# One pass of matmuls for values and row sums in a perceiver block: halves aligned by small transfers, the product moved to other engines, the mask spread by TensorE

## The chip, the cores and the metric

The kernel runs on one core of a Trainium2 chip. The metric is the time of one execution on the device in microseconds (us). The engines are PE (TensorE; PEld is its weight load), DVE (VectorE), ACT (ScalarE), POOL (GpSimd) and SP (SyncE, which here only issues transfers). Each runs its own instructions strictly in order; they meet through semaphores.

## The reference

64 sequences of 64 queries, model width 128, 16 heads of 8. Only the first 64 of the 128 context rows count, because of the causal mask. Three layers, each added to x:

```python
# layer one: cross attention on layernorm(x), keys and values from ctx
scores = einsum('bhqd,bhkd->bhqk', Q, K) / sqrt(8); scores = where(mask == 0 or k > q, -inf, scores)
x = x + softmax(scores) @ V, heads joined, @ Wo
# layer two: self attention on layernorm(x), keys and values through a latent of 32
scores = clip(q k / sqrt(128), -1e4, 1e4) * exp(-1e-4 * |q - k|)
x = x + softmax(scores) @ V, heads joined, @ Wo
# layer three: feed-forward on layernorm(x), 128 -> 512 -> 128, GELU, inputs and weights rounded to 127 steps
```

## The kernel before

A **tile** is 128 rows of x: two sequences of 64 queries. There are 32 tiles (`NT`) in each attention layer, numbered 0 to 31 in layer one and 32 to 63 in layer two (`NS` = 64). The program is a software pipeline written out by hand: each engine has its own loop over **turns** n, and in turn n an engine works on tile n for the early steps and on older tiles for the late ones. `due(n, lags)` says which tile a step has in turn n. The order inside a turn is the order of the lines in each engine's loop, and an engine that waits holds up all that stands behind the wait.

In turn n of layer one:

- PE: `scores(n)` (L560) into four banks of PSUM (the accumulators); `values` of tile n-3, which is 16 small matmuls with the values as weights (L606, numerator) and then 8 with a table of ones (L612, the sums of the exponentials, spread over the same partitions); `project` of tile n-4 (L622, with Wo); `to_keys(n-2)`, eight transposes in two halves (L579); then one "piece", mostly a projection of four tiles (kinds q, k, v, x; L474, L487, L495, L458). fp32 matmuls other than transposes show as two instructions each.
- DVE: scale the scores and add the mask (L1027); `add_residual` of tile n-4 (L962), which waits for `project`; the row maxima (L1046); `divide` of tile n-3 (L968), the product of numerator and inverse sum, which gives `oT`, the input of `project`; moments for a later layernorm (L938, L942).
- POOL: subtract the maxima (L408, 128x1024); later in layer one also a normalisation (`normalise`, L329).
- ACT: logarithm of the sum (L834), exponentials of tile n-2 in two halves (L829) with the inverse of the sum, exp(-log), between them (L840), then the copy of the piece out of PSUM (L786, L778, L797, L772).

In layer two the lags of `values` and `project` are one turn longer; DVE clips (L1032) and takes maxima in two halves (L1041, L1043); POOL multiplies by the decay (L400, 128x1024) and subtracts the maxima of half the heads (L408, 128x512); PE subtracts the other half itself (`shift_keys`, L591), into the bank of the second half of the transposes, whose exponential ACT takes first in the next turn.

The banks for `project`, the transposes and the pieces form a ring of three (`NR`), in the order of the list `order`: who comes three places later waits until the bank has been read. Numerator and sums share the bank `OB`. Every fourth turn SP spreads new keys over `kx` with four transfers (L305). The mask is loaded for all 128 partitions and made by POOL in eight groups (`make_mask`, L364 and L367).

## Time and profile before

| | |
|---|---|
| median of 3 runs | 310.81 us (310.68 to 311.25) |
| the profiled execution | 311.19 us, span of the profile 309.4 us |
| busy: PE, DVE, ACT, POOL | 285.5, 255.9, 219.6, 209.9 us |
| first and last L1027 (layer one) | 10.1 and 129.0 us |
| first and last L1032 (layer two) | 132.8 and 252.2 us |

Layer one and layer two take the span from about 10 to 260 us, and layer three the rest. An engine's busy time says how full it is; which of the engines sets the length of a turn is read from waits and from the order of the instructions.

### The profile page before, as it was taken

To read this page: it belongs to the slowest core of one execution; us is meant where nothing else is said; L and a number is where in the kernel's file an instruction comes from. 1 tells how busy PE (TensorE), PEld (TensorE's weight loads), DVE (VectorE), ACT (ScalarE), POOL (GpSimd) and SP (SyncE) were. 2 spreads that over 40 slices of the span, in tenths; PEclk is the share of its full clock that TensorE was granted. 3 is DMA by queue.
4 is the path that set the end of the run, shared out by engine and by line. 5 is a ranking of instruction groups with operands and counts; after the bars stand their busy time and mean duration, and the time that the engine had idled before them with its cause. 6 is when DMAs were issued, how large, how long until landed. Compare 5 with 4: busy or idle time off the path is not lost.

```text
span 309.4 us, 13624 instructions
## 1 busy us (share of the span) xinstructions
PE 285.5 (92%) x5744; PEld 197.6 (64%) x5744; DVE 255.9 (83%) x558; ACT 219.6 (71%) x496; POOL 209.9 (68%) x167
## 2 busy tenths in 40 slices
PE   7789879999999999999999999999999999699593
PEld 2356547676767777675767686777777768332282
DVE  2898679999888888888888787878888998789873
ACT  3585856575768876666777778788857877699590
POOL 5676557777877766799999998988799962230000
PEclk9999999999999999999999999999999999999869
DMA  8999000101010000000000000000000000000027
GB/s 229 313 286 298 12 28 4 36 2 40 2 37 9 31 19 20 28 14 24 17 33 6 21 20 21 19 21 20 11 31 5 2 5 4 0 0 0 2 78 195
DMA packets 19038, 15.05 MB, mean 49 GB/s; under 512 B 5985, under 2 KB 15522, under 8 KB 18978
## 3 DMA queue, kind: packets, MB, share of 16 engines
q1 hardware_dynamic: 18258, 13.75, 15.5%
q8 instruction: 46, 0.75, 1.1%
q10 hardware_dynamic: 720, 0.43, 0.5%
q14 instruction: 14, 0.11, 0.1%
HBM read 8.67 MB, written 2.10 MB: 35 GB/s over the span
## 4 chain that ended last, share of the span: by engine, by line
PE 73%; DVE 15%; issue 4%; DMA 3%; ACT 2%; POOL 1%; SPq 1%; DVEq 0%; ACTq 0%; POOLq 0%
PE ps L579 12%; PE ps L560 11%; PE ps L606 10%; PE ps L612 8%; PE ps L622 8%; DVE hmax L1108 6%; PE ps L577 4%; PE ps L495 4%; PE ps L487 4%; PE ps L474 3%; PE ps L591 3%; DVE u L1027 3%; PE ps L718 2%; DMA arena<-in_mask_BxS_if 2%; DMA out<-pt 1%
## 5 line engine op out<-in xcount | busy, mean ns | idle before, releaser
L829 ACT ACTIVATE pt<-ps 128x512 f32<-128x512 f32 x128 | 76.0, 595 | 30.5 <-PE ps L579 23.3
L408 POOL TENSOR_TENSOR u<-u,mx 128x1024 f32<-128x1024 f32 x32 | 60.8, 1902 | 35.3 <-DVE mx L1046 35.1
L400 POOL TENSOR_TENSOR ud<-u,con 128x1024 f32<-128x1024 f32 x31 | 73.4, 2367 | 6.6 <-DVE u L1032 6.5
L1027 DVE SCALAR_TENSOR_TENSOR u<-ps,rs,arena 128x1024 f32<-128x1024 f32 x32 | 40.9, 1279 | 14.1 <-PE ps L560 12.7
L1032 DVE TENSOR_SCALAR u<-ps 128x1024 f32<-128x1024 f32 x32 | 39.0, 1220 | 11.8 <-PE ps L560 11.3
L560 PE MATMUL ps<-arena,qT 32*64 32x256 f32 x1024 | 44.0, 399 | 4.9 <-DVE u L1027 2.5
L606 PE MATMUL ps<-pt,vx 128*32 128x64 f32 x2048 | 41.4, 221 | 2.9 <-DVE oT L968 1.3
L606 PEld LDWEIGHTS ps<-pt,vx 128*32 128x32 f32 x2048 | 32.5, 110 | 16.4 <-issue 11.5
L612 PE MATMUL ps<-pt,con 128*32 128x128 f32 x1024 | 40.0, 273 | 0.7 <-issue 0.7
L1046 DVE TENSOR_REDUCE mx<-u 128x16 f32<-128x1024 f32 x32 | 38.7, 1210 | 0.1
L834 ACT ACTIVATE lden<-ps 128x128 f32<-128x128 f32 x64 | 17.7, 277 | 29.5 <-PE ps L612 29.4
L560 PEld LDWEIGHTS ps<-arena,qT 32*64 32x64 f32 x1024 | 14.9, 129 | 31.2 <-issue 21.6
L579 PE MATMUL ps<-con,u 128*128 128x128 f32 x256 | 33.3, 273 | 0.0
L408 POOL TENSOR_TENSOR ud<-ud,mx 128x512 f32<-128x512 f32 x30 | 31.3, 1043 | 2.4
L622 PE MATMUL ps<-wo,oT 128*128 128x128 f32 x128 | 31.3, 326 | 0.7 <-DVE oT L968 0.7
L938 DVE BATCH_NORM_STATS2 stats<-x 128x6 f32<-128x128 f32 x96 | 25.7, 280 | 5.4 <-DMA x<-in_x 5.2
L579 PEld LDWEIGHTS ps<-con,u 128*128 128x128 f32 x256 | 28.9, 141 | 0.6 <-issue 0.6
L622 PEld LDWEIGHTS ps<-wo,oT 128*128 128x128 f32 x128 | 19.0, 188 | 13.3 <-issue 12.1
L962 DVE TENSOR_TENSOR x<-ps,x 128x128 f32<-128x128 f32 x64 | 18.5, 290 | 10.7 <-PE ps L622 10.5
L797 ACT COPY vx<-ps 64x256 f32<-64x256 f32 x64 | 23.4, 366 | 4.9 <-PE ps L495 4.0
L612 PEld LDWEIGHTS ps<-pt,con 128*32 128x32 f32 x1024 | 25.9, 110 | 1.0 <-issue 1.0
L1041 DVE TENSOR_REDUCE mx<-u 128x8 f32<-128x512 f32 x32 | 21.6, 676 | 0.2
(153 smaller groups left out, 513.5 us busy)
## 6 DMA issues: line engine op xcount, KB each, us to landing
arena<-kT SPq DMA_DIRECT2D x52, 64.0 KB, 2.2
out<-pt SPq DMA_DIRECT2D x8, 256.0 KB, 2.8
arena<-in_ctx_cols SPq DMA_DIRECT2D x4, 256.0 KB, 4.5
xn3T<-in_x_cols SPq DMA_DIRECT2D x4, 256.0 KB, 4.6
x<-in_x SPq DMA_DIRECT2D x4, 256.0 KB, 5.2
arena<-in_ctx_cols SPq DMA_DIRECT2D x2, 512.0 KB, 6.3
xn3T<-in_x_cols SPq DMA_DIRECT2D x2, 512.0 KB, 6.0
x<-in_x SPq DMA_DIRECT2D x2, 512.0 KB, 7.3
```

The source lines that it names most:

```text
L400: pool.tensor_tensor(dh, uh, decay.unsqueeze(1).to_broadcast([P, H, HALF]), ALU.mult)\
L408: pool.tensor_tensor(uh, uh, mx[:, n % 4, 0:count].unsqueeze(2).to_broadcast([P, count, HALF]), ALU.subtract)\
L560: last = pe.matmul(ps[HALF * b:HALF * (b + 1), r].rearrange("p (h k) -> p h k", h=HR)[:, :, 0:HALF], qT[rows, j % RING3, i * P + HALF * b: ...
L579: last = pe.transpose(out_t, in_t, ident)
L606: pe.matmul(ps[32 * r:32 * (r + 1), bank, HALF * b:HALF * (b + 1)], vx[:, j % RING3, b, i, r].rearrange("p c m -> p (c m)")[:, 16 * par:16 ...
L612: last = pe.matmul(ps[32 * r:32 * (r + 1), bank, P:2 * P], ones[:, par], pt[:, n % 2, 2 * r + par, :], start=(par == 0), stop=(par == 1))
L622: pe.matmul(ps[:, bank, 0:D], oT[:, n % 2], wo[:, layer], start=True, stop=True)\
L829: act.activation(pt[:, n % 2, 4 * half:4 * half + 4].rearrange("p h n -> p (h n)"), ps[:, bank, :], ACT.Exp).then_inc(s["emptied"], 1)
L938: dve.bn_stats(stats[:, k, t % 4], x[:, t]).then_inc(ST[k], 1)
L1027: dve.scalar_tensor_tensor(by_head(u[:, n % UB]), sc, rs[:, 0, n:n + 1], mask[:, n].unsqueeze(1).to_broadcast([P, H, HALF]), ALU.mult, ALU ...
L1032: dve.tensor_scalar(by_head(u[:, n % UB]), sc, CLAMP, -CLAMP, ALU.min, ALU.max)\
L1046: dve.tensor_reduce(mx[:, n % 4], by_head(u[:, n % UB]), AX.X, ALU.max)\
```

## The change

`values` no longer runs its second set of 8 matmuls (L612), except in the last two tiles. The weights of the first set become 32 columns wide with values and ones in turn, so that 16 matmuls give numerator and sum together: in one half of the bank the numerators stand on even partitions and the sums on odd ones, in the other half the reverse (the last two tiles keep the old way with weights of their own, `vl`). So that numerator and sum stand on the same partition, ACT copies the bank out (`take_out`, 128x256 into `raw`), and SP starts four transfers between partitions for each tile (`align`, 64 partitions x 512 bytes each, `raw` to `nd`). The logarithm of a tile waits for its two transfers `D_IN`, the product for `N_IN`, and both come one turn later than before (`LAG_DEN`), as do `project` and `add_residual`. `values` waits for the copy of the tile before (`raw_done`), no longer for its product.

The product of tiles 0 to 31 is made by POOL, behind the subtraction of its turn; that of tiles 32 to 61 by DVE, with the inverse sum in PSUM. The mask is loaded for two partitions only, made into bf16 by DVE, and spread and joined with the causal part by PE (piece `m`, 8 tiles at a time, copied out by ACT). The ones in the weights are set once, by DVE and POOL at the start. Some turns of layer three's layernorm move by one.

```diff
+LAG_T, LAG_SHIFT, LAG_PV, LAG_DEN = 2, 3, (3, 4), (4, 5)
+WHOLE = NS - 2
+def den_turn(n):
+    return n + (LAG_PV[1] if n >= WHOLE else LAG_DEN[n // NT])
+def divided(turn):
+    return [n for n in range(NS) if den_turn(n) == turn]
+def added(turn):
+    return [n for n in range(NS) if den_turn(n) + 1 == turn]
...
+        def product_made(eng, n):
+            eng.wait_ge(s["o_first" if n < NT else "o_ready"], n % NT + 1)
...
+            def align(n):
+                slot = n % RAW
+                sp.wait_ge(s["raw_done"], n + 1)
+                if n >= RAW:
+                    product_made(sp, n - RAW)
+                sp.dma_start(nd[0:P:2, slot, 1], raw[1:P:2, slot, 0]).then_inc(D_IN[slot], 16)
+                sp.dma_start(nd[1:P:2, slot, 1], raw[0:P:2, slot, 1]).then_inc(D_IN[slot], 16)
+                sp.dma_start(nd[0:P:2, slot, 0], raw[0:P:2, slot, 0]).then_inc(N_IN[slot], 16)
+                sp.dma_start(nd[1:P:2, slot, 0], raw[1:P:2, slot, 1]).then_inc(N_IN[slot], 16)
...
 # POOL, behind the subtraction of turn n
-                for m, (turn, _, _, _) in enumerate(MAKE):
-                    if turn == n:
-                        make_mask(m)
+                for tile in divided(n):
+                    if tile < NT:
+                        divide(tile)
...
 # PE
                 if 1 <= n < NS - 1:
-                    pe.wait_ge(s["o_ready"], n)
+                    pe.wait_ge(s["raw_done"], n)
+                if NT + 2 <= n < NS - 1:
+                    product_made(pe, n - 2)
+                if n < WHOLE:
+                    for b in range(2):
+                        for par in range(2):
+                            for r in range(RG):
+                                last = pe.matmul(ps[32 * r:32 * (r + 1), bank, P * par + HALF * b:P * par + HALF * (b + 1)],
+                                                 vx[:, j % RING3, b, i, r, 32 * par:32 * (par + 1)],
+                                                 pt[:, n % 2, 2 * r + par, HALF * b:HALF * (b + 1)], start=True, stop=True)
+                    last.then_inc(s["pv_done"], 1)
+                    return
...
 # ACT
+            def take_out(n):
+                act.wait_ge(s["pv_done"], n + 1)
+                if n >= RAW:
+                    act.wait_ge(D_IN[n % RAW], aligned(n - RAW))
+                    act.wait_ge(N_IN[n % RAW], aligned(n - RAW))
+                act.copy(raw[:, n % RAW].rearrange("p a n -> p (a n)"), ps[:, OB, 0:2 * P])\
+                    .then_inc(s["raw_done"], 1)
+
             def log_den(n):
-                act.wait_ge(s["pv_done"], n + 1)
-                act.activation(lden[:, n % 2], ps[:, num_den(n), P:2 * P], ACT.Ln).then_inc(s["ln_done"], 1)
+                if n < WHOLE:
+                    act.wait_ge(D_IN[n % RAW], aligned(n))
+                    act.activation(lden[:, n % 2], nd[:, n % RAW, 1], ACT.Ln).then_inc(s["ln_done"], 1)
...
 # DVE
+            dve.wait_ge(s["mask_in"], 16)
+            dve.tensor_scalar(mask_b[:, :], mask_i, 0.0, MASKED, ALU.is_equal, ALU.mult).then_inc(s["mask_cast"], 1)
             for t in range(GT):
                 moments(0, t)
...
-                for tile in due(n, LAG_ADD):
+                for tile in added(n):
                     add_residual(tile)
...
-                for tile in due(n, LAG_PV):
-                    if tile not in (EARLY, NS - 1):
+                for tile in divided(n):
+                    if NT <= tile < NS - 1:
                         divide(tile)
```

Three places of the new order follow. First POOL, around turns 15 to 18 of layer one. Before, behind the splitting of a bias:

```order
L346 CAST b2h<-b2d 1x128 [waits b2_split]
L408 TENSOR_TENSOR u<-u,mx 128x1024 [waits maxed] x3
L329 TENSOR_SCALAR xn3T<-x,mv,rs 128x128 [waits rs1]
L408 TENSOR_TENSOR u<-u,mx 128x1024 [waits maxed]
L329 TENSOR_SCALAR xn3T<-x,mv,rs 128x128 [waits rs1]
```

And now (`nd` lies in the tensor arena; L480 is the subtraction, L406 the product):

```order
L427 CAST b2h<-b2d 1x128 [waits b2_split]
L480 TENSOR_TENSOR u<-u,mx 128x1024 [waits maxed]
L406 TENSOR_TENSOR oT<-arena,rden 128x128 [waits wo_done,n_in0,den_ready]
L480 TENSOR_TENSOR u<-u,mx 128x1024 [waits maxed]
L406 TENSOR_TENSOR oT<-arena,rden 128x128 [waits wo_done,n_in1,den_ready]
L480 TENSOR_TENSOR u<-u,mx 128x1024 [waits maxed]
L406 TENSOR_TENSOR oT<-arena,rden 128x128 [waits wo_done,n_in2,den_ready]
L410 TENSOR_SCALAR xn3T<-x,mv,rs 128x128 [waits rs1]
```

A product stands behind each subtraction; the one in turn n is that of tile n-4. Second DVE, one turn of layer one (scores, addition of tile n-4, maxima, product of tile n-3, moments) before:

```order
L1027 SCALAR_TENSOR_TENSOR u<-ps,rs,arena 128x1024 [waits s_done,rs0,filled]
L962 TENSOR_TENSOR x<-ps,x 128x128 [waits wo_done]
L1046 TENSOR_REDUCE mx<-u 128x16 [waits s_read]
L968 TENSOR_TENSOR oT<-ps,rden 128x128 [waits wo_done,den_ready]
L938 BN_STATS stats<-x 128x6 [waits mv1,x_added]
L942 BN_AGGR mv<-stats 128x2 [waits st1]
```

And now:

```order
L1156 SCALAR_TENSOR_TENSOR u<-ps,rs,arena 128x1024 [waits s_done,rs0,filled]
L1086 TENSOR_TENSOR x<-ps,x 128x128 [waits wo_done]
L1175 TENSOR_REDUCE mx<-u 128x16 [waits s_read]
L1062 BN_STATS stats<-x 128x6 [waits mv1,x_added]
L1066 BN_AGGR mv<-stats 128x2 [waits st1]
```

The product is gone from DVE, and the addition, now of tile n-5, still stands ahead of the maxima. Third ACT, one turn of layer one before:

```order
L834 ACTIVATE lden<-ps 128x128 [waits pv_done]
L829 ACTIVATE pt<-ps 128x512 [waits pv_done,filled]
L840 ACTIVATE rden<-lden 128x128 [waits o_ready,ln_done]
L829 ACTIVATE pt<-ps 128x512 [waits filled]
L846 ACTIVATE w1r<-w1r,cst,scal 128x512 [waits wscale]
```

And now:

```order
L946 ACTIVATE lden<-arena 128x128 [waits d_in1]
L940 COPY arena<-ps 128x256 [waits n_in2,d_in2,pv_done]
L932 ACTIVATE pt<-ps 128x512 [waits pv_done,filled]
L956 ACTIVATE rden<-lden 128x128 [waits o_first,ln_done]
L932 ACTIVATE pt<-ps 128x512 [waits filled]
```

The logarithm of one tile, which waits for transfers, now stands ahead of the copy that starts the transfers of the next.

## Rows read from the trace of the kernel before

**Rows 1.** The page's busy times and its chain that ended last.

```profile
PE 285.5 (92%) x5744; PEld 197.6 (64%) x5744; DVE 255.9 (83%) x558; ACT 219.6 (71%) x496; POOL 209.9 (68%) x167
...
PE 73%; DVE 15%; issue 4%; DMA 3%; ACT 2%; POOL 1%; SPq 1%; DVEq 0%; ACTq 0%; POOLq 0%
```

**Rows 2.** Busy time in stretches: layer one, then four turns of layer two.

```profile
50.00:80.00 30.00, 29.70 (x611) 20.80 (x599) 29.09 (x72) 18.93 (x53) 24.10 (x27) 1.00 0.06 21
...
165.54:181.35 15.81, 15.77 (x378) 11.46 (x376) 13.19 (x34) 11.97 (x30) 14.69 (x11) 1.00 0.07 21
```

**Rows 3.** Timeline of layer two: ACT, PE and PEld in one turn.

```profile
182.56 0.60 ACT L829 ACTIVATE pt<-ps 128x512 f32<-128x512 f32 x1 [0.38 <-PE ps L591]
182.79 0.61 PE L612 MATMUL ps<-pt,con 128*32 128x128 f32 x16
183.33 0.49 PE L622 MATMUL ps<-wo,oT 128*128 128x128 f32 x2
183.54 0.47 PEld L579 LDWEIGHTS ps<-con,ud 128*128 128x128 f32 x4
...
185.51 0.23 PEld L560 LDWEIGHTS ps<-arena,qT 32*64 32x64 f32 x16
```

**Rows 4.** Groups by line: busy, mean ns, idle before.

```profile
L612 PE MATMUL ps<-pt,con 128*32 128x128 f32 x1024 | 40.0, 273 | 0.7 <-issue 0.7
L797 ACT COPY vx<-ps 64x256 f32<-64x256 f32 x64 | 23.4, 366 | 4.9 <-PE ps L495 4.0
L387 POOL TENSOR_TENSOR wkv_raw<-wkv_raw 128x128 f32<-128x128 f32 x1 | 0.5, 463 | 0.0
```

**Rows 5.** Timeline of layer one: PE, DVE and POOL in one turn.

```profile
99.71 0.49 PE L622 MATMUL ps<-wo,oT 128*128 128x128 f32 x2
100.24 0.29 DVE L962 TENSOR_TENSOR x<-ps,x 128x128 f32<-128x128 f32 x1
100.45 1.21 DVE L1046 TENSOR_REDUCE mx<-u 128x16 f32<-128x1024 f32 x1
101.74 1.90 POOL L408 TENSOR_TENSOR u<-u,mx 128x1024 f32<-128x1024 f32 x1 [1.12 <-DVE mx L1046]
103.63 0.79 POOL L329 TENSOR_SCALAR xn3T<-x,mv,rs 128x128 f32<-128x128 f32 x1
```

**Rows 6.** Timeline of DVE: the additions of turns 8 and 31.

```profile
44.00 0.29 DVE L962 TENSOR_TENSOR x<-ps,x 128x128 f32<-128x128 f32 x1
...
130.29 0.29 DVE L962 TENSOR_TENSOR x<-ps,x 128x128 f32<-128x128 f32 x1
```

**Rows 7.** Timeline of POOL: decays of turns 35, 36, 40, 41 and 62.

```profile
147.35 2.37 POOL L400 TENSOR_TENSOR ud<-u,con 128x1024 f32<-128x1024 f32 x1
150.80 2.38 POOL L400 TENSOR_TENSOR ud<-u,con 128x1024 f32<-128x1024 f32 x1
...
165.08 2.38 POOL L400 TENSOR_TENSOR ud<-u,con 128x1024 f32<-128x1024 f32 x1
169.01 2.37 POOL L400 TENSOR_TENSOR ud<-u,con 128x1024 f32<-128x1024 f32 x1
...
250.06 2.37 POOL L400 TENSOR_TENSOR ud<-u,con 128x1024 f32<-128x1024 f32 x1
```

**Rows 8.** Key transfers: issue time and time to landing, at 84 and 99 us.

```profile
L305 SPq DMA_DIRECT2D arena<-kT x4: 459/594/1687, 84.1 to 86.9; - x4
DMA to landing us min/median/max: 1.9/2.6/3.0
...
DMA to landing us min/median/max: 1.8/1.9/1.9
```

**Rows 9.** Timeline of the start: what the first scores wait for.

```profile
7.57 1.41 DVE L1012 TENSOR_SCALAR arena<-kT,con 128x512 f32<-128x512 f32 x3
7.92 1.32 POOL L364 TENSOR_SCALAR arena<-arena 128x256 f32<-128x256 int32 x1 [3.26 <-DMA arena<-in_mask_BxS_if]
10.11 1.28 DVE L1027 SCALAR_TENSOR_TENSOR u<-ps,rs,arena 128x1024 f32<-128x1024 f32 x1 [1.12 <-POOL arena L367]
```

More of the change, by code:

```diff
@@ L104, in ring_plan @@
         pieces[n] += these
+    for c in range(1, NT // MASK_TILES):
+        pieces[MASK_TURN[c]].append(("m", c))
     for n in range(NS):
@@ L116, in ring_plan @@
         keys = [("t", turn - LAG_T, half) for half in range(2)] if 0 <= turn - LAG_T < NS else []
-        order += [("o", n) for n in due(turn, LAG_ADD)] + keys + pieces[turn]
+        order += [("o", n) for n in added(turn)] + keys + pieces[turn]
         by_act += [("t", n, 1) for n in [turn - LAG_SHIFT] if NT <= n < NS] + (keys if turn - LAG_T < NT else keys[:1]) + pieces[turn]
@@ L224, in perceiver_block @@
         KX_IN = [s[f"kx_in{n}"] for n in range(RING3)]
-        MASK_IN = [s[f"mask_in{n}"] for n in range(4)]
+        N_IN, D_IN = [s[f"n_in{n}"] for n in range(RAW)], [s[f"d_in{n}"] for n in range(RAW)]
         STORED = [s[f"stored{n}"] for n in range(4)]
@@ L261, in gelu_count, with aligned, columns_of @@
             return 1 + max(m for m, e in enumerate(GELUS) if e[0] == k)
+        def aligned(n):
+            return 32 * (n // RAW + 1)
+        def columns_of(v, slot, e, first, between):
+            pitch, blocks = v.shape[1] * v.shape[2] * v.shape[3] * RG * VW, v.shape[3] * RG
+            return [bass.AP(v[:, :, :, :, :, :].tensor, HALF * e * pitch + (2 * slot + b) * blocks * VW + 2 * DH * e + first,
+                            [[pitch, HALF], [VW, blocks], [between, 2], [2, DH]]) for b in range(2)]
         def gets_empty(what):
@@ L772, in piece @@
                     last = act.copy(xT[:, j % 2], ps[:, bank, :])
+                if kind == "m":
+                    last = act.copy(mask[:, j * MASK_TILES:(j + 1) * MASK_TILES].rearrange("p t k -> p (t k)"), ps[:, bank, :])
                 if kind == "cq":
@@ L1033, in _ @@
                         .then_inc(s["clipped"], 1)
-                for tile in due(n, LAG_ADD):
+                for tile in added(n):
                     add_residual(tile)
@@ L1160 @@
             a = a[:, spread]
+        if name in _OF_VALUES:
+            a = a[by_turns]
         a = _np.ascontiguousarray(a)
```

196 lines of the change are left out of this document (128 added, 68 removed).

## The prediction

> **What bounds the kernel now.** I read the page first: PE is busy 92% of the span and holds 73% of the chain that ended last, DVE 83% [rows 1]. That is an average, so the stretches come next. In layer one, from 50 to 80 us, PE is busy 29.70 of 30 us and DVE 29.09; in four turns of layer two PE is busy 15.77 of 15.81 us, POOL 14.69, DVE 13.19, ACT 11.97 [rows 2]. So PE sets the turn in both layers: 15.81 / 4 = 3.95 us in these turns of layer two, and (130.29 - 44.00) / 23 = 3.75 us over the additions of turns 8 to 31 in layer one [rows 6]. Next behind PE stand DVE in layer one and POOL in layer two. The question for a change that lightens PE is thus what the next engines allow, and whether a new order ties them together.
>
> **What is removed.** The second set of matmuls is busy 40.0 us in all [rows 4], and in the turn shown it begins at 182.79 and `project` at 183.33, so 0.54 us of PE's time a turn goes [rows 3]. The first set keeps its number, its 64 columns and its 32-column weights; I cost its new form at nothing. On PE alone layer one would fall to 3.75 - 0.54 = 3.21 us a turn.
>
> **What it costs in layer one: a ring of waits over four engines.** In turn n POOL now makes the product of tile n-4 behind its subtraction of tile n. `project` of tile n-4 on PE (turn n+1) needs this product. `add_residual` of the same tile on DVE (turn n+1) needs `project`, and it stands ahead of the maxima of tile n+1. The subtraction of tile n+1 on POOL needs these maxima, and the next product stands behind that subtraction. So each turn has to pass once through: `project` to addition, 99.71 to 100.24, 0.53 us; addition to maxima, 0.21; maxima to the start of the subtraction, 100.45 to 101.74, 1.29; subtraction to the next instruction of POOL, 101.74 to 103.63, 1.89 [rows 5]; the product; and the hand-over to PE. Before, the product stood on DVE right behind the maxima, and the subtraction was in no such ring.
>
> The product on POOL is not in the trace. The nearest row is POOL's tensor_tensor of the same shape and type, 0.46 us [rows 4], and I take that. The lower bound, from the 1.90 us for 1024 columns [rows 5] and a straight line through 0.46 for 128, cannot be much less; I put 0.40. The upper bound is the 0.79 us of POOL's tensor_scalar of this shape [rows 5]. For the hand-over I take what POOL needed after the end of the maxima, 101.66 to 101.74, 0.08 us [rows 5]. Sum: 0.53 + 0.21 + 1.29 + 1.89 + 0.46 + 0.08 = 4.46 us. No other ring or engine is longer: PE would need 3.21, and DVE's 29.09 of 30 us, 3.64 a turn [rows 2], loses a product of about the addition's 0.29 [rows 5]. PE waits in front of `project`, with the transposes, the piece and the next scores queued behind. 23 turns at 4.46 are 102.6 us against 86.3 [rows 6]: **+16.3 us**.
>
> The Trainium skill speaks against this placement: GPSIMD Engine Reference, section 4.1, advises VectorE for elementwise work and calls GpSimd about 2x slower with two inputs. The trace shows 0.46 against the 0.29 us of DVE's addition of the same shape, 1.6 times. By the page's factor the product would take 0.58 us and the ring 4.58, an estimate, which makes the end 2.8 us later than my sum.
>
> **The start.** The mask is now cast on DVE ahead of the first moments. The old mask reached POOL at 7.92 us; I let the new one land then too. The cast is 2048 columns on two partitions; three of 512 columns took 1.41 us [rows 9], so 4 x 0.47 = 1.9 us. The moments and the three L1012 operations come behind it. The first L1027 started at 10.11 after 1.12 us of waiting for the old mask [rows 9], so its scores were there at 8.99; pushed back by 1.9 (only the cast) to 3.3 us (also the wait for the landing), it starts at 10.9 to 12.3. Some of this is absorbed in the uneven first turns. At turn 8 I take +1.7 us, bounds +0.5 and +3.
>
> **From layer one into layer two.** Addition of turn 8: 44.0 + 1.7 = 45.7; of turn 31: 148.3; of turn 32: 152.8. Its product was done 0.61 us earlier (0.08 + 0.53), at 152.1. From there POOL runs without a pause up to the decay of tile 36: four turns of decay and subtraction at 3.45 us (147.35 to 150.80 [rows 7]) with a product of 0.46 each, three normalisations of 0.79 [rows 5], and one pair of small layernorm steps, 0.48 (165.08 to 169.01 against 3.45 [rows 7]). 152.1 + 15.6 + 2.4 + 0.5 = 170.6. Before it was 150.80 [rows 7]: **+19.8 us** by then.
>
> **Layer two.** Products are back on DVE, behind the maxima, so the ring is open. The transposes use a bank of the ring of three whose last reader is the exponential that ends at 182.56 + 0.60 = 183.16; they began at 183.54 [rows 3]. Of PE's 0.54 us only 0.38, less a hand-over of 0.08, can be taken: 3.95 - 0.30 = 3.65. POOL needs 3.45, or 3.57 with the small steps every fourth turn [rows 7]. In the last turns there are fewer pieces, so POOL's figure holds there. I take 3.58 over the 26 turns from the decay of tile 36 to that of tile 62, 93.1 us, against 250.06 - 150.80 = 99.3 [rows 7]: **-6.2 us**. Bounds: 3.50 (91.0) and no gain (99.3).
>
> Costed at nothing there, with the cover named: ACT's copy of 128x256 out of PSUM, about 0.37 us [rows 4], brings ACT to 11.97 + 1.5 = 13.5 of 14.3 us in four turns, so ACT has hardly any cover left. SP's issues, 0.59 us each [rows 8]: four a turn and one for the keys, 3.0 us, under a turn. The transfers: the second of a pair lands 1.9 us after its issue [rows 8]. The tail from turn 63 has the lags of before, and layer three is the same: 0.
>
> **Sum.** Against the profiled execution of 311.19 us: 311.2 + 19.8 - 6.2 = 324.8. The median of the runs lies 0.4 below that execution, so 324.4 us.
>
> **Rivals.**
> A, the other side: the ring of layer one doesn't close, and the lighter PE decides. Then layer one runs at DVE's 3.64 - 0.29 = 3.35 us, 9.2 us less over 23 turns; the start costs 1.7, the four products on POOL after it 1.8, layer two gives 6.2: 310.8 - 9.2 + 1.7 + 1.8 - 6.2 = 299 us. For it: PE has most work, and POOL sits idle 1.12 us before the subtraction shown [rows 5]. Against it: that idle time lies ahead of the subtraction, not behind it, and the product is behind it. It decides once the ring is under 3.75 us, 0.7 less than the rows give. Chance 0.10.
> B: a second ring, through the transfers, sets layer two. ACT's logarithm of a tile waits for its sums and stands ahead of the copy that starts the next tile's transfers: copy 0.37, hand-over 0.08, first issue 0.59, landing of the second 1.9, hand-over 0.08, logarithm at most 0.37: 3.4 us [rows 4, 8], hidden. But in one group of four the landings took 2.6 and up to 3.0 us, and one issue 1.69 [rows 8]; at 2.6 the ring is 4.1 us, and 26 turns give 13.5 us more than I forecast: 338 us. In layer one 4.46 hides it. Against it: the other group shown landed in 1.9 throughout. Chance 0.12.
> C: the ring is there, but layer two gains nothing (ACT full): 330.6 us. Chance 0.08, inside the range.
> My forecast has 0.70.
>
> **How the numbers follow.** Predicted 324.4, the likeliest case. Bounds down: product 0.40 (-1.4), start (-1.2), layer two (-2.1): 319.7. Up: product 0.79 (+7.6 in layer one, +1.3 in turns 32 to 35) gives 333.3, start +1.3. Reaching a little beyond, and leaving out most of A and B, the range is 316 to 335. About 0.2% is what a measurement of this kernel can tell from no change. Faster is A with a scrap of the forecast's ring falling short, 0.12; between lies almost nothing, 0.02; slower 0.86.
>
> **What the profile after would show.** The first steps are right if PE's busy time falls by some 35 us and its share drops well below 90% in layer one, with PE idle ahead of `project`, released by POOL's `oT`; if additions in layer one stand 4.4 to 4.5 us apart; if POOL's product takes 0.4 to 0.5 us and starts at the end of the subtraction; if layer two's decays stand 3.5 to 3.6 apart. I am wrong if POOL's product starts well after the subtraction (it then waits for N_IN or the inverse, and the transfers decide), if additions in layer one are 3.3 to 3.8 apart (A), or if ACT sits idle for D_IN ahead of the logarithm in layer two (B).

## The result and the profile after

The changed kernel takes 340.97 us (median of 4 runs, 339.24 to 343.85), the kernel before 310.75 us on the same chip (4 runs, 309.7 to 311.25). The ratio is 1.098, with a 95% interval of 1.094 to 1.102. I had predicted 324.4 us and a range of 316 to 335. The direction and the reason for most of the loss were right, but the time was 16.6 us too low and outside the range. The profiled execution took 339.24 us, with a span of 337.4. Executions over 1.5% above the fastest of the same kernel count as slow (up to half of the executions of a kernel below, none of the changed kernel's four); the medians and ratios here leave them out, the ranges hold them.

The page of the kernel after: busy time, the chain that ended last by engine and by line, and the groups that count.

```profile
PE 270.9 (80%) x4760; PEld 183.4 (54%) x4760; DVE 253.6 (75%) x529; ACT 235.7 (70%) x566; POOL 212.5 (63%) x197
...
POOL 25%; issue 18%; PE 14%; DMA 11%; SPq 11%; ACT 10%; DVE 10%; POOLq 0%; DVEq 0%; ACTq 0%
...
L716 PE MATMUL ps<-wo,oT 128*128 128x128 f32 x128 | 31.8, 333 | 34.0 <-POOL oT L406 28.0
...
L946 ACT ACTIVATE lden<-arena 128x128 f32<-128x128 f32 x62 | 19.2, 310 | 24.8 <-DMA arena<-arena 24.3
```

PE did lose work (285.5 us before, 270.9 now), but it no longer holds 73% of the chain as in [rows 1]: it has 14%. The chain now goes round through POOL, DVE, the transfers and the queue that issues them (SPq). PE sits idle 34.0 us in front of `project` (L716 in this kernel), 28.0 of them for POOL's `oT`.

The timeline of the kernel after, from 122 to 127 us in layer one, shows the ring. The columns are start, duration, engine and line, and in brackets the idle time before the instruction with what ended it.

```profile
122.26 0.49 PE L716 MATMUL ps<-wo,oT 128*128 128x128 f32 x2 [1.40 <-POOL oT L406]
122.78 0.29 DVE L1086 TENSOR_TENSOR x<-ps,x 128x128 f32<-128x128 f32 x1 [1.02 <-PE ps L716]
122.99 1.21 DVE L1175 TENSOR_REDUCE mx<-u 128x16 f32<-128x1024 f32 x1
124.28 1.90 POOL L480 TENSOR_TENSOR u<-u,mx 128x1024 f32<-128x1024 f32 x1 [1.31 <-DVE mx L1175]
126.14 0.46 POOL L406 TENSOR_TENSOR oT<-arena,rden 128x128 f32<-128x128 f32 x1
126.65 0.49 PE L716 MATMUL ps<-wo,oT 128*128 128x128 f32 x2 [0.94 <-POOL oT L406]
```

Every step starts as soon as the one before it ends, over four engines: 0.52 + 0.21 + 1.29 + 1.86 + 0.51 = 4.39 us from one `project` to the next. In [rows 5] the same maxima and subtraction stand with 1.12 us idle ahead of the subtraction, but nothing behind it fed `project`.

Stretches of the kernel after: layer one from turn 8 to 31, layer two from the clip of turn 37 to that of turn 63, and the tail from there to the joint maximum of layer three. Then follow the same three of the kernel before. The columns are the window and its length, busy time of PE, PEld, DVE, ACT and POOL (with counts), the granted clock, the DMA engines' share, and GB/s.

```profile
44.92:147.28 102.36, 80.94 (x1448) 55.58 (x1441) 73.56 (x142) 68.37 (x181) 64.93 (x68) 0.97 0.15 45
174.29:275.78 101.49, 92.51 (x2067) 67.16 (x2055) 83.70 (x193) 80.17 (x216) 90.79 (x64) 1.00 0.17 50
275.78:296.62 20.84, 14.12 (x267) 11.14 (x265) 14.50 (x47) 12.75 (x38) 4.37 (x6) 0.86 0.09 24
```

```profile
42.73:129.02 86.29, 85.46 (x1812) 61.07 (x1804) 77.04 (x165) 59.55 (x156) 62.27 (x54) 1.00 0.06 18
150.74:252.18 101.44, 101.07 (x2480) 74.46 (x2472) 85.56 (x196) 77.28 (x187) 92.38 (x64) 1.00 0.05 16
252.18:268.00 15.82, 13.99 (x331) 10.79 (x320) 14.10 (x42) 11.78 (x30) 4.74 (x8) 1.00 0.01 3
```

Three things can be read from the two tables. Layer one lost 16.1 us over 23 turns (3.75 to 4.45 us a turn), while PE had 4.5 us less to do: its idle time grew from 0.8 to 21.4 us. In layer two PE has 8.6 us less to do, and the stretch is not a bit shorter (101.49 against 101.44): PE is idle 9 us where it was idle 0.4. And the tail is 5.0 us longer with hardly more work in it (PE 14.12 us against 13.99).

The timeline of the kernel after in layer two, from 204 to 212 us, shows what PE waits for there. SPq rows are transfers being issued (L341 and L342 move sums, L343 and L344, not shown here, numerators).

```profile
204.75 1.48 SPq L342 DMA_DIRECT2D arena<-arena  x1
...
207.46 0.31 ACT L946 ACTIVATE lden<-arena 128x128 f32<-128x128 f32 x1 [1.47 <-DMA arena<-arena]
...
209.00 1.62 ACT L898 COPY vx<-ps 64x256 f32<-64x256 f32 x4
210.64 0.60 ACT L932 ACTIVATE pt<-ps 128x512 f32<-128x512 f32 x1
211.38 0.63 PE L662 MATMUL ps<-con,ud 128*128 128x128 f32 x4 [1.01 <-ACT pt L932]
```

A slow issue (1.48 us where most take 0.60), whose transfer lands 2.7 us after the start of that issue, holds up ACT's logarithm by 1.47 us. ACT's own queue (a copy, two exponentials, a normalisation, four copies of values) passes the delay on, and at 211.38 PE waits 1.01 us for an exponential. From 174 to 275 us, in the totals of the waits, the logarithm waits for a transfer 10.8 us in 13 places, and DVE's product 8.5 us in 7. Of the 26 second transfers of the sums there, 9 landed later than 2.4 us after the start of their issue, up to 3.3; the fastest took 1.8.

### The profile page after: what moved, and what is told of

Its sections match the earlier page's. It is cut to its first block, busy times and chain, and to the rows that moved or that the text cites. A ratio compares the mean times of both kernels' runs of the same rounds, so it can differ in the third digit from the quotient of the medians.

```text
span 337.4 us, 12133 instructions
## 1 busy us (share of the span) xinstructions
PE 270.9 (80%) x4760; PEld 183.4 (54%) x4760; DVE 253.6 (75%) x529; ACT 235.7 (70%) x566; POOL 212.5 (63%) x197
## 3 DMA queue, kind: packets, MB, share of 16 engines
q1 hardware_dynamic: 33940, 20.86, 20.4%
## 4 chain that ended last, share of the span: by engine, by line
POOL 25%; issue 18%; PE 14%; DMA 11%; SPq 11%; ACT 10%; DVE 10%; POOLq 0%; DVEq 0%; ACTq 0%
POOL u L480 14%; DMA arena<-arena 9%; DVE hmax L1237 5%; POOL xn3T L410 4%; POOL oT L406 3%; SPq L341 3%; PE ps L812 3%; ACT vx L898 2%; SPq L362 2%; SPq L343 2%; ACT pt L932 2%; SPq L342 2%; DMA arena<-in_mask_BxS_if 2%; PE ps L643 1%; PE ps L662 1%
## 5 line engine op out<-in xcount | busy, mean ns | idle before, releaser
L480 POOL TENSOR_TENSOR u<-u,mx 128x1024 f32<-128x1024 f32 x32 | 60.8, 1902 | 55.7 <-DVE mx L1175 55.7
L716 PE MATMUL ps<-wo,oT 128*128 128x128 f32 x128 | 31.8, 333 | 34.0 <-POOL oT L406 28.0
L643 PE MATMUL ps<-arena,qT 32*64 32x256 f32 x1024 | 45.0, 408 | 4.0 <-ACT arena L925 2.6
L692 PEld LDWEIGHTS ps<-pt,vx 128*32 128x32 f32 x1984 | 31.8, 110 | 25.1 <-ACT pt L932 10.6
L716 PEld LDWEIGHTS ps<-wo,oT 128*128 128x128 f32 x128 | 19.6, 193 | 42.4 <-POOL oT L406 33.4
L946 ACT ACTIVATE lden<-arena 128x128 f32<-128x128 f32 x62 | 19.2, 310 | 24.8 <-DMA arena<-arena 24.3
L662 PE MATMUL ps<-con,u 128*128 128x128 f32 x256 | 34.2, 278 | 0.0
L480 POOL TENSOR_TENSOR ud<-ud,mx 128x512 f32<-128x512 f32 x30 | 31.3, 1043 | 2.4
L662 PEld LDWEIGHTS ps<-con,u 128*128 128x128 f32 x256 | 29.8, 145 | 0.6 <-issue 0.4
L898 ACT COPY vx<-ps 64x256 f32<-64x256 f32 (+1 forms) x64 | 24.8, 388 | 3.8 <-PE ps L578 2.8
L940 ACT COPY arena<-ps 128x256 f32<-128x256 f32 x62 | 22.5, 363 | 4.5 <-PE ps L692 3.7
L662 PE MATMUL ps<-con,ud 128*128 128x128 f32 x128 | 19.7, 276 | 3.6 <-ACT pt L932 2.6
```

The costliest lines, as they stand in the source:

```text
L480: pool.tensor_tensor(uh, uh, mx[:, n % 4, 0:count].unsqueeze(2).to_broadcast([P, count, HALF]), ALU.subtract)\
L643: last = pe.matmul(ps[HALF * b:HALF * (b + 1), r].rearrange("p (h k) -> p h k", h=HR)[:, :, 0:HALF], qT[rows, j % RING3, i * P + HALF * b: ...
L662: last = pe.transpose(out_t, in_t, ident)
L692: last = pe.matmul(ps[32 * r:32 * (r + 1), bank, P * par + HALF * b:P * par + HALF * (b + 1)], vx[:, j % RING3, b, i, r, 32 * par:32 * (pa ...
L716: pe.matmul(ps[:, bank, 0:D], oT[:, n % 2], wo[:, layer], start=True, stop=True)\
L898: last = act.copy(blocks[b][:, 0:whole * RG], src[:, 0:whole * RG])
```

## The experiments

Each ran beside the kernel before, whose medians were 310.7 to 311.0 us; the ratio is to that. The first figure is the median. Layer one below is the time of a turn from turn 8 to 31, layer two from the clip of turn 37 to that of turn 63, and the tail the time from there to the joint maximum. All three are from one profiled execution of each kernel, so differences of a few tenths of a us in the tail, or of 0.05 us a turn, are no more than a hint: e10 has the tail of e8, and yet 0.7 us more.

| kernel | us (lowest to highest) | ratio, 95% | layer one | layer two | tail |
|---|---|---|---|---|---|
| before | 310.75 | 1 | 3.75 | 3.90 | 15.8 |
| after | 340.97 (339.24-343.85) | 1.094-1.102 | 4.45 | 3.90 | 20.8 |
| e1_product_first | 328.21 (327.19-329.56) | 1.053-1.064 | 4.08 | 3.94 | 20.5 |
| e2_product_twice | 354.96 (353.83-359.4) | 1.138-1.150 | 4.84 | 4.04 | 20.6 |
| e3_maxima_first | 346.49 (344.33-351.25) | 1.106-1.126 | 4.77 | 4.07 | 20.4 |
| e4_copy_first | 338.15 (334.62-340.84) | 1.078-1.094 | 4.39 | 3.81 | 20.4 |
| e5_both | 314.85 (313.73-320.6) | 1.008-1.021 | 3.79 | 3.80 | 20.6 |
| e6_keys_late | 316.76 (313.46-318.35) | 1.009-1.024 | 3.63 | 3.83 | 21.0 |
| e7_half_transfers | 335.49 (334.94-340.97) | 1.075-1.088 | 4.39 | 3.82 | 20.6 |
| e8_last_three | 313.12 (309.1-314.96) | 1.001-1.009 | 3.67 | 3.86 | 18.9 |
| e10_keys_sooner | 311.46 (310.34-312.47) | 0.998-1.003 | 3.62 | 3.81 | 19.7 |
| e11_no_align | 303.71 (302.74-304.39) | 0.974-0.979 | 3.53 | 3.71 | 18.5 |
| e12_after_no_align | 329.25 (328.5-329.52) | 1.056-1.061 | 4.44 | 3.70 | 18.4 |
| e13_tail_order | 309.73 (307.14-315.0) | 0.996-1.001 | 3.65 | 3.73 | 18.5 |

**e1_product_first.** POOL makes the product of the turn ahead of the subtraction, not behind it. This opens the ring without taking any work away.

```diff
             for n in TURNS:
+                for tile in divided(n):
+                    if tile < NT:
+                        divide(tile)
                 if n < NS - 1:
...
-                for tile in divided(n):
-                    if tile < NT:
-                        divide(tile)
```

> The product of layer one stands on POOL ahead of the subtraction of its turn, nothing else is changed. Ring theory (project, addition, maxima, subtraction, product set layer one's turn of 4.39 us): the ring opens, additions in layer one come 3.5 to 3.9 us apart, layer one gets 12 to 18 us shorter, 323 to 329 us in all. Rival (the transfers or the full ACT set layer one's turn and POOL's product only waits with them): 4.3 to 4.4 us apart as before, 339 to 342 us. Layer two stays at 3.90 us a turn by both.

The time fell by 12.8 us with the same instructions, so the ring had been the bound of layer one. But the turn stopped at 4.08 us. The waits of this kernel from 60 to 138 us (total, times, longest) say why:

```profile
POOL oT L406 <- ACT rden L956: 20.0, 17, 2.4
ACT lden L946 <- DMA arena<-arena: 19.5, 11, 2.4
```

Behind the first ring stood the second, rival B's: ACT copies the sums out, SP issues the transfers, they land, and ACT, waiting for them with the logarithm, has the next tile's copy queued behind it. I had put that ring at 3.4 us. Here the mean turn took 4.08, with the additions 3.4 to 5.2 us apart: the second ring holds up some turns and not others. The time is in the range of the ring theory, the turn is not (3.5 to 3.9), since that theory left the second ring out.

**e2_product_twice.** POOL makes the product twice, first into a scrap buffer.

```diff
+                pool.tensor_tensor(scrap[:, :], nd[:, n % RAW, 0], inverse(n), ALU.mult)
                 pool.tensor_tensor(oT[:, n % 2], nd[:, n % RAW, 0], inverse(n), ALU.mult).then_inc(s["o_first"], 1)
```

> Each product of layer one is made twice on POOL, the first time into scratch that nobody reads. Ring theory: each turn of layer one grows by one product, 0.42 to 0.46 us, over 27 turns and the four after it: 12 to 14 us more, 353 to 355 us. Rival (POOL's product is not in what sets the turn): under 2 us more, 341 to 343 us.

The timeline of POOL in this kernel:

```profile
103.56 1.90 POOL L482 TENSOR_TENSOR u<-u,mx 128x1024 f32<-128x1024 f32 x1 [1.29 <-DVE mx L1177]
105.42 0.45 POOL L407 TENSOR_TENSOR scrap<-arena,rden 128x128 f32<-128x128 f32 x1
105.83 0.45 POOL L408 TENSOR_TENSOR oT<-arena,rden 128x128 f32<-128x128 f32 x1
106.27 0.79 POOL L412 TENSOR_SCALAR xn3T<-x,mv,rs 128x128 f32<-128x128 f32 x1
108.36 1.90 POOL L482 TENSOR_TENSOR u<-u,mx 128x1024 f32<-128x1024 f32 x1 [1.30 <-DVE mx L1177]
```

The kernel takes 14.0 us more than the changed one, as expected. From one subtraction to the next it is 4.80 us, 0.41 more than 4.39, and 0.41 is what the added product takes from its start to the next start. An engine that is busy 65 of 102 us passes on all of what it is given, because the product stands in the ring. The normalisation behind the product (0.79 us) isn't in the ring and costs nothing.

**e3_maxima_first.** The other way of opening the ring: in layer one DVE takes the maxima ahead of the addition.

```diff
-                for tile in added(n):
-                    add_residual(tile)
+                if n >= NT:
+                    for tile in added(n):
+                        add_residual(tile)
...
+                if n < NT:
+                    for tile in added(n):
+                        add_residual(tile)
```

> In layer one the addition stands behind the maxima on DVE. Ring theory: the addition leaves the ring, and what is left is the way scores, maxima, subtraction, product, project, next scores but one, about 8.0 us for two turns: 4.0 us a turn, layer one 9 us shorter, 332 us. Rival (the way over the addition is not what sets the turn): 4.39 us as before, 339 to 342 us.

This missed: 346.49 us, slower still than the changed kernel (the intervals of their ratios don't overlap). The timeline of this kernel shows a new ring in place of the old one:

```profile
96.78 0.28 DVE L1086 TENSOR_TENSOR x<-ps,x 128x128 f32<-128x128 f32 x1
...
97.20 1.10 PE L570 MATMUL ps<-arena,wk 128*128 128x512 f32 x2 [1.14 <-DVE x L1086]
98.23 0.69 PE L643 MATMUL ps<-arena,qT 32*64 32x256 f32 x16
...
99.12 1.28 DVE L1156 SCALAR_TENSOR_TENSOR u<-ps,rs,arena 128x1024 f32<-128x1024 f32 x1 [1.74 <-PE ps L643]
...
100.44 1.22 DVE L1176 TENSOR_REDUCE mx<-u 128x16 f32<-128x1024 f32 x1
101.58 0.28 DVE L1086 TENSOR_TENSOR x<-ps,x 128x128 f32<-128x128 f32 x1
```

PE's piece uses the bank in which `project` left its result three places earlier, so it waits for the addition. The next scores stand behind the piece, their reading by DVE behind the scores, the maxima behind that, and the addition now behind the maxima: 96.78 to 101.58, 4.80 us. The addition stood first because it frees a bank, and that I hadn't seen.

**e4_copy_first.** On ACT the copy of a tile's sums and numerators (`take_out`) goes ahead of the logarithm of the tile before it, so that its transfers start without waiting for those of that tile.

```diff
-                for tile in divided(n):
-                    if tile < WHOLE:
-                        log_den(tile)
                 for tile in due(n, LAG_PV):
                     if tile < WHOLE:
                         take_out(tile)
+                for tile in divided(n):
+                    if tile < WHOLE:
+                        log_den(tile)
```

> On ACT the copy out of PSUM stands ahead of the logarithm of the older tile in both layers. Transfer ring theory for layer two (logarithm waits for its transfers and holds back the copy that starts the next ones): layer two falls from 3.90 to 3.6 us a turn, and the last tiles come sooner, 8 to 12 us less, 329 to 333 us. Rival one (SP's queue of four to six issues a turn sets layer two): little change in layer two, 0 to 3 us less. Rival two (ACT is simply full): no change. Layer one stays at 4.39 by all of them.

A gain of 2.8 us between the medians, which is not clear of the scatter (the intervals of the ratios of this and the changed kernel touch), and 3.90 to 3.81 us a turn in layer two. That is what rival one had, 0 to 3 us, and not the 8 to 12 of the transfer ring. Opening this ring didn't bring the turn to 3.58, nor to 3.6.

**e5_both.** Both edits, e1 and e4, together.

> Product of layer one ahead of the subtraction and, on ACT, the copy ahead of the logarithm: e1 and e4 together. In e1 layer one ran at 4.08 us a turn with ACT waiting 19.5 us for transfers ahead of the logarithm. Transfer ring theory: with the ring over POOL open as well, layer one falls to 3.4 to 3.7 us a turn and layer two to 3.8 (as in e4): 308 to 318 us. Rival (SP's queue alone sets layer one after e1): still about 4.0 in layer one, 322 to 326 us.

314.85 us. Together the two edits give more than the sum of what each gives: e1 alone 12.8 us, e4 alone 2.8, both 26.1. With the first ring opened the second was the bound of layer one, and e4 removes that (4.08 to 3.79), though not down to the 3.4 to 3.7 expected.

**e6_keys_late.** In addition SP issues the four key transfers one per turn and behind the aligning ones, where they had been two per turn and ahead of them.

```diff
-                    for h0 in (0, 2):
-                        if n == GT * j - SPREAD + h0 // 2:
-                            spread(j, h0)
...
+                    for h in range(HR):
+                        if n == GT * j - SPREAD + h:
+                            spread(j, h)
```

> e5 with SP's four issues for the keys one in each turn and behind that turn's four, in place of two in each of two turns and ahead of them. SP queue theory: two turns of four held six issues of 0.6 us and now none holds more than five, so layer two falls from 3.81 to about 3.65 us a turn and layer one by 0 to 0.1: 3 to 6 us below e5. Rival (ACT's order and the landings alone are left): within 1.5 us of e5.

No gain in the medians (316.76 against 314.85, intervals that overlap), which is nearer to the rival than to the queue theory. In the profiled executions layer one is quicker (3.79 to 3.63), layer two is not. The wait moved: over the whole run the logarithm waits 11.1 us for transfers where it waited 22.3 in e5, and the weight load of the scores now waits 10.0 us in 9 places for the keys, where it had not waited.

**e7_half_transfers.** The changed kernel without the two transfers of numerators; the product reads the numerators as they lie, so what comes out is not the reference's result.

```diff
-                sp.dma_start(nd[0:P:2, slot, 0], raw[0:P:2, slot, 0]).then_inc(N_IN[slot], 16)
-                sp.dma_start(nd[1:P:2, slot, 0], raw[1:P:2, slot, 1]).then_inc(N_IN[slot], 16)
```

> The changed kernel with only the two transfers for the sums; the product reads the unaligned copy, so odd partitions multiply a sum in place of a numerator (that part of the computation is left wrong in value, not in work). SP issues two in place of four a turn for a tile. SP queue theory for layer two: 3.90 falls to 3.6 to 3.7, and the last tiles no longer wait for the numerator's landing, 8 to 12 us less in all. Transfer ring theory (the logarithm waits and holds back the copy; it needs only the first two): 3.90 falls by no more than 0.1, 0 to 3 us less, and 1 to 3 more in the last tiles. Layer one stays at 4.4 by both, as POOL's product is not touched.

5.5 us less than the changed kernel between the medians. In the one profiled execution, which was only 0.8 us shorter than that of the changed kernel, layer two fell from 3.90 to 3.82 us a turn, the tail by 0.3 us, and layer one kept its ring (4.39). Layer two moved by what the transfer ring theory had, at most 0.1, and half the transfers gone brought it no lower than e4's reordering did (3.81).

**e8_last_three.** e6, and three tiles at the end take the old way in two sets of matmuls, where it was two (`WHOLE = NS - 3`).

> e6 with three tiles in place of two at the end made in the old way (own sums on PE, no transfers), lden moved into free space of the arena. Theory: in the changed kernel the last product but two waited until 288.0 us for its transfer with PE idle behind it, and then the clock granted to PE fell to 0.61; with one aligned tile less this wait moves one turn earlier, where PE still has work: 1 to 3 us less than e6. Rival (the wait stays whole at the next tile): same as e6 within 1 us.

313.12 us, 3.6 less than e6; the tail went from 21.0 to 18.9 us, in the range that the theory gave. The granted clock was no part of it: over the tail it was 0.92 in e6 and 0.91 here. With 19.7 us in e10, whose tail has the same instructions, the gain from where the last tile goes that is sent through the transfers is 1.3 to 2.1 us.

**e10_keys_sooner.** e8, with the keys' issues begun one turn sooner (`SPREAD = 6`).

> The three edits and the earlier end of the last run, with the keys' four issues begun one turn sooner. Theory that late keys are what layer two still waits for: the 10 us that the scores' weight load waits for kT falls to under 4, layer two from 3.86 to about 3.75 us a turn, and the time to 1 to 3 us below that of the last run, about 311. Rival, that the aligning transfers and PE's own work hold layer two: within 1 us of the last run, 313 to 314, with layer two at 3.82 to 3.90.

311.46 us, 1.7 less than e8, and the weight load of the scores no longer waits for the keys (in e8 it did so 11.7 us in 10 places). The time is what the theory of late keys wanted, but layer two, 3.86 to 3.81 us a turn, fell less than it wanted. The intervals of the ratios of e8 and e10 overlap a little. The kernel is now level with the one before.

**e11_no_align** and **e12_after_no_align.** No aligning transfer at all, in e6 and in the changed kernel. The product reads the unaligned tile as soon as it is copied out; the logarithm reads as many numbers of it, with scale 0 and a positive bias, so that its result is a constant. What comes out is not the reference's result.

```diff
-                sp.dma_start(nd[0:P:2, slot, 1], raw[1:P:2, slot, 0]).then_inc(D_IN[slot], 16)
-                sp.dma_start(nd[1:P:2, slot, 1], raw[0:P:2, slot, 1]).then_inc(D_IN[slot], 16)
-                sp.dma_start(nd[0:P:2, slot, 0], raw[0:P:2, slot, 0]).then_inc(N_IN[slot], 16)
-                sp.dma_start(nd[1:P:2, slot, 0], raw[1:P:2, slot, 1]).then_inc(N_IN[slot], 16)
...
-                    act.activation(lden[:, n % 2], nd[:, n % RAW, 1], ACT.Ln).then_inc(s["ln_done"], 1)
+                    act.activation(lden[:, n % 2], raw[:, n % RAW, 1], ACT.Ln, bias=cst[:, 3:4], scale=0.0).then_inc(s["ln_done"], 1)
```

> Beside the run with product first, copy first and keys late (317.3 us). No aligning transfer is issued at all: the product reads the unaligned tile, and the logarithm reads the same amount of data of that tile with scale 0 and a positive bias, so its result is a constant; the numbers that come out are not the reference's. All arithmetic instructions keep number and size. Theory that the transfers (their landings, and the queue that issues them) hold layer two at 3.8 us a turn: it falls to 3.6, and the stretch from the last clip of layer two to the maxima of layer three from 21 to 16 or 17 us; time 306 to 309. Rival, that PE's and ACT's own work holds it: layer two stays at 3.75 or more, time over 312.

> The changed kernel, without any aligning transfer, as in the run beside it (product and logarithm read the unaligned tile, the logarithm with scale 0 and a positive bias; the numbers that come out are not the reference's). The ring through POOL is still closed, so by my theory layer one stays at 4.38 to 4.45 us a turn; layer two falls from 3.90 to 3.6 us a turn (8 us) and the tail by 4 to 5 us, in all 327 to 331 against 341. If the transfers had no part in the misses of layer two and of the tail, the time stays within 3 us of 341; if they also set layer one, it falls below 325.

These price the transfers. The same three stretches of e12_after_no_align:

```profile
43.04:145.08 102.04, 79.66 (x1448) 55.39 (x1440) 73.36 (x142) 70.11 (x181) 64.93 (x68) 0.98 0.04 15
172.08:268.19 96.11, 91.43 (x2063) 66.91 (x2054) 83.03 (x193) 82.42 (x215) 88.75 (x63) 1.00 0.05 17
268.19:286.64 18.45, 13.02 (x284) 10.07 (x273) 14.52 (x47) 13.42 (x39) 6.12 (x8) 1.00 0.01 3
```

Layer one doesn't move (102.04 us against 102.36), so behind the closed ring the transfers have no part in its 4.45 us a turn. Layer two loses 5.4 us and the tail 2.4; the start loses 0.5, the first eight turns 1.4 and layer three 0.7. The total, 11.7 us between the medians, and layer one are as my theory had them, but layer two stopped at 3.70 us where I had written 3.6, and the tail lost 2.4 us and not 4 to 5. e11_no_align says the same with the rings open (3.71), though its time fell below both theories' figures (306 to 309, and over 312), its layer two lies between them (3.6, and 3.75 or more) and its tail above the 16 or 17 us of the first: layer one gained as well, 3.63 to 3.53. At 303.71 us it shows what a free alignment would be worth: 2.3% under the kernel before, or a little more, since the logarithm with scale and bias takes 0.39 us where it took 0.31.

**e13_tail_order.** e10, with two blocks of DVE's work in the last turns moved back, behind the product and the addition of the last tile.

```diff
-                if n == APPLY3[5]:
+                if n == APPLY3[5] + 1:
                     last_norm(5, range(20, 24))
...
-                if n == NS - 1 + LAG_PV[1]:
+                if n == NS + LAG_PV[1]:
                     dve.wait_ge(s["xn3_pool"], 1)
```

> The best version so far (311.5 us), with two blocks of VectorE's work in the last turns moved back: the normalisation and maximum of the sixth group of layer three behind the product of the last tile, and the maximum of the seventh behind the addition of the last tile. In the last run the last product began at 264.64 us though its inverse was ready at 262.55, behind 1.16 + 0.60 us of that normalisation and maximum. Theory that this order is a part of the tail's loss: last product at about 262.8 us of that run's clock, the final maxima 1.5 to 2 us sooner, limited then by GpSimd's last normalisation, which ended at 266.25; time 309.5 to 310.2, just under the kernel before. Rival, that the last normalisation's own inputs decide: within 0.5 us of 311.5.

The timelines of DVE, from the last clip to the last product and the joint maximum, first of e10_keys_sooner and then of e13_tail_order:

```profile
249.57 1.22 DVE L1163 TENSOR_SCALAR u<-ps 128x1024 f32<-128x1024 f32 x1
...
264.64 0.27 DVE L1096 TENSOR_TENSOR oT<-ps,rden 128x128 f32<-128x128 f32 x1
...
269.22 0.16 DVE L1221 TENSOR_REDUCE scal<-amax 128x1 f32<-128x8 f32 x1
```

```profile
246.58 1.21 DVE L1163 TENSOR_SCALAR u<-ps 128x1024 f32<-128x1024 f32 x1
...
259.60 0.27 DVE L1096 TENSOR_TENSOR oT<-ps,rden 128x128 f32<-128x128 f32 x1
...
265.12 0.16 DVE L1221 TENSOR_REDUCE scal<-amax 128x1 f32<-128x8 f32 x1
```

The last product of e13 comes 13.0 us behind the last clip and not 15.1, and the joint maximum 18.5 and not 19.7. How much of these 1.1 us is the order isn't shown, as the granted clock over the tail was 0.91 in e10 and 1.00 in e13. The median, 309.73 us, lies in the range of the theory; it is the lowest of the versions with the alignment, and 0.4% under the kernel before, but the interval of the ratio includes 1: it can't be told from the kernel before. The idea, with its rings opened, only breaks even.

## Why the prediction was right in layer one and wrong behind it

**PE's relief (0.54 us a turn): too large.** PE's timeline in the kernel before and after, in a turn of layer two with the same piece behind it; the rows are `values` (in the kernel before also the set of sums, which follows 0.45 us later, in [rows 3]) and `project`.

```profile
182.34 0.62 PE L606 MATMUL ps<-pt,vx 128*32 128x64 f32 x32
```

```profile
205.17 0.65 PE L692 MATMUL ps<-pt,vx 128*32 128x64 f32 x32
205.75 0.49 PE L716 MATMUL ps<-wo,oT 128*128 128x128 f32 x2
```

Before, from the first matmul of values to `project` it was 182.34 to 183.33, 0.99 us; after, 0.58. The relief is 0.41 us a turn. I had taken the time from the start of the second set to `project`, 0.54, but the second set starts while the first still runs, and without it that overlap of 0.13 us goes too. Over a whole turn it is less still, 0.31 to 0.35 us, as the lines under layer two below show. And in e11, with both rings open and no transfers, PE is busy 79.80 of 81.24 us of layer one at 3.53 us a turn, where I had 3.21 for PE. PE's busy time as a whole fell by 14.6 us and not by the 35 that I gave as a sign. None of this is in the miss, though: in layer one the ring decides, and in layer two my sum took only 0.30 us of the 0.54.

**The ring of layer one: right.** Additions stand 4.39 to 4.40 us apart in undisturbed turns, where I wrote 4.46 (that the mean of the 23 turns, 4.475, comes closer is luck: turns of 5.79 and 4.86 us lift it); the product takes 0.46 us, the value I took from the 128x128 row of POOL, and the hand-over 0.05. The addition of turn 31 starts at 149.16 us against 148.3. e1 (opened, -12.8 us) and e2 (0.41 us more in it, 14.0 us slower) show that it is the ring and not a full engine. The Trainium skill (GPSIMD Engine Reference, section 4.1) counts GpSimd as about 2x slower with two inputs, which would have given 0.58 us for the product, an estimate; the trace has 0.46 against DVE's 0.29, 1.6 times.

**The start and the way into layer two: right, by a reading that was wrong.** The first scores were read at 12.42 us, just over my 10.9 to 12.3. That the scores of the kernel before were there at 8.99 was misread: from 8.99 DVE was free, and the scores' matmuls only began at 9.21, behind the three operations L1012. The cast moved these (L1142 now) from 7.57 to 9.73 us, which is 2.2 of the 2.3 us, and the scores' matmuls began at 11.05, right behind them. The addition of turn 8 came 2.2 us later than before, where I took 1.7. From the addition of turn 31 to the decay of tile 36 it was 23.1 us, forecast 22.3.

**Layer two, 3.58 us a turn and 6.2 us won: this is the step that failed, together with the tail.** It measured 100.6 us between the decays of tiles 36 and 62 (172.24 to 272.86), 7.5 over the forecast of 93.1. I gave the turn to POOL, hid the ring through the transfers (rival B) with a landing of 1.9 us, and costed ACT's part at nothing. Two waits stood in its place.

The first is the transfers. ACT sits idle ahead of the logarithm, the sign that I had named for B. Rows that pointed to it were already in [rows 8]: landings of 2.6 and 3.0 us and an issue of 1.69 among eight. They are no rare case here: a third of the 26 landings that I followed took over 2.4 us. A ring of 3.4 us in a turn of 3.6 has 0.2 us to give, and a single late landing costs more. Between the same two decays e12_after_no_align takes 97.4 us (170.02 to 267.45), so 3.2 of the 7.5 us are the transfers'.

The other 4.3 stay without them: 3.75 us a turn, with PE busy 95% of the stretch and POOL 92%. Here PE waits for ACT, always in the same place. The timeline of e12_after_no_align, one turn behind a piece of values (L574), which ACT copies out with four copies (L894):

```profile
202.61 0.63 PE L658 MATMUL ps<-con,ud 128*128 128x128 f32 x4
...
203.51 1.06 PE L574 MATMUL ps<-wv,xT 128*128 128x128 f32 x8
204.60 1.63 ACT L894 COPY vx<-ps 64x256 f32<-64x256 f32 x4 [0.35 <-PE ps L574]
205.94 0.49 PE L712 MATMUL ps<-wo,oT 128*128 128x128 f32 x2
206.25 0.60 ACT L928 ACTIVATE pt<-ps 128x512 f32<-128x512 f32 x1
207.00 0.63 PE L658 MATMUL ps<-con,ud 128*128 128x128 f32 x4 [0.57 <-ACT pt L928]
```

And the kernel before at the same place:

```profile
183.65 0.60 PE L579 MATMUL ps<-con,ud 128*128 128x128 f32 x4
...
187.35 0.49 PE L622 MATMUL ps<-wo,oT 128*128 128x128 f32 x2
187.88 0.63 PE L579 MATMUL ps<-con,ud 128*128 128x128 f32 x4
```

The transposes need the bank that this exponential reads, and the exponential stands behind the four copies. So from one set of transposes to the next it is 4.39 us in this turn (202.61 to 207.00), 4.23 before: in every fourth turn the lighter PE gains nothing. In the three others it gains 0.31 to 0.35 (before 4.02, 3.99 and 3.56, now 3.67, 3.67 and 3.25). The six such turns of the stretch hold 3.6 us of PE waiting for that exponential, where the waits of the kernel before list none; without them the 97.4 us would be 93.8, against my 93.1. My 0.30 us a turn was read behind a piece of another kind, [rows 3], and taken for all turns. In the kernel before the wait showed only as 0.53 us from `project` to the transposes in four of the six turns behind a piece of values, with 0.33 in the other turns. No run took the copies out of the exponential's way, so this price comes from the waits and not from an experiment.

Neither rival B (4.1 us a turn all through, 338 us) nor rival C (ACT full; it is busy 82 of 96 us in e12) is what happened, though the mechanism of each strikes in some turns.

**The tail, costed at nothing: wrong by 5.2 us.** The last tile that goes through the transfers has no work left to hide them. The timeline of the kernel after:

```profile
284.74 0.60 SPq L344 DMA_DIRECT2D arena<-arena  x1
...
288.02 0.29 DVE L1094 TENSOR_TENSOR oT<-arena,ps 128x128 f32<-128x128 f32 x1 [2.10 <-DMA arena<-arena]
...
288.37 0.71 PE L716 MATMUL ps<-wo,oT 128*128 128x128 f32 x4 [1.75 <-DVE oT L1094]
```

This transfer, the second of the numerators of tile 61, took 3.2 us from issue to landing. Then come two stretches of the tail, behind that product:

```profile
289.00:291.00 2.00, 0.51 (x5) 0.28 (x3) 1.97 (x6) 0.81 (x4) 1.52 (x2) 0.94 0.00 0
291.00:297.00 6.00, 4.64 (x17) 3.56 (x18) 4.39 (x18) 3.87 (x9) 2.64 (x4) 0.50 0.01 4
```

PE had been idle for 1.75 us ahead of 288.37 and was busy only 0.5 us from 289 to 291; from 291 to 297 the granted clock was 0.50, the lower of its two levels (1.2 of 2.4 GHz), where before it stood at 1.00 over the whole tail. It was below 1.00 over the tail in every version with transfers but e13, and 1.00 in both without. From the decay of tile 62 to the end it is 64.5 us, before 59.3, and in e12_after_no_align 59.3 again, with the clock at 1.00. So, cut at that decay, the transfers account for the whole of this term, the lower clock included; what the clock alone cost isn't shown. (Cut at clips, as in the table, the shares are 5.4 us for layer two and 2.4 for the tail, because the last clip itself comes 2.92 us after that decay in the kernel after and 0.74 in e12. Either way the transfers cost 8.5 us from the decay of tile 36 to the end, 0.7 of it in layer three.)

**The sum.** The forecast span was 323.0 us, the measured one 337.4. The difference of 14.4 is 0.9 up to the addition of turn 31, 0.8 from there to the decay of tile 36, 7.5 in layer two and 5.2 behind it. The other 2 us between my 324.4 and the median of 340.97 are mostly that this median lies 1.7 us above the profiled execution, where before it lay 0.4 below.

## What to carry to other kernels

Write down each ring (which instruction waits for which, once round to the same one) before moving an operation between engines: here a product of 0.46 us on an engine with a third of its time free cost 16 us, since it closed a loop over four engines. With both rings opened, the same instructions in another order cost layer one nearly nothing (3.79 against 3.75 us). A second ring that a first one hides counts too: undoing one gave 12.8 us, the other 2.8, both 26.1. A relief read in one turn holds for the turns of that kind: every fourth turn here had another wait behind it. A ring through transfers needs room for late landings, not for the median one, and at the end of a pipeline, where nothing covers them, they are paid in full.

## What was not expected of the hardware

- Landings of the same transfer within one run scatter: 1.8 us at best, 9 of 26 over 2.4, up to 3.3 in the kernel after, though the DMA engines are busy only 17% in that stretch. In each of the 9 turns with a late landing, that transfer's issue or one of the next two on the queue took 1.1 to 1.9 us, and only one other turn of the stretch has an aligning issue as slow: late landings and slow issues come together. Why isn't shown. Two or three rows of before were too few to see how often it happens.
- A transfer costs SP 0.47 us to issue when the queue had been waiting and 0.60 behind another, but single ones took 1.1 to 1.9 us. Six a turn, 3.6 us, leave nothing of a turn of 3.7 us.
- Matmuls of two sets overlap across the border between them, so the time that a set takes between two starts (0.54 us) is not what its removal gives (0.41 up to `project`, 0.31 to 0.35 over a whole turn).
